# Sending each token once, to its pair of experts, in the last mixture of a vision tower

## The reference, cut to what matters

```python
def _L1_ffn_ref(x, gate_w, gate_b, w1, b1, w2, b2):
    B, S, H, E, K = (8, 1024, 128, 8, 2)
    logits = jnp.einsum('bsh,he->bse', x, gate_w) + gate_b
    topk_vals, topk_idx = jax.lax.top_k(logits, K)
    topk_weights = jax.nn.softmax(topk_vals, axis=-1)
    mask = jax.nn.one_hot(topk_idx, E, dtype=topk_weights.dtype)
    weights = jnp.einsum('bske,bsk->bse', mask, topk_weights)
    h = jax.nn.relu(jnp.einsum('bsh,ehf->bsef', x, w1) + b1)
    expert_out = jnp.einsum('bsef,efh->bseh', h, w2) + b2
    return jnp.einsum('bseh,bse->bsh', expert_out, weights)
...
h = h + _L1_ffn_ref(_layernorm(h, axis=-1), ...)
```

## Time and profile before

| | |
|---|---|
| median of three runs | 1982.61 us |
| the profiled execution: span from its first to its last instruction | 2111.4 us |
| of that: start of the last stage | 1570.6 us |
| routing and wait for the first block | 1570.6 to 1817.8 us |
| blocks, to the last scatter | 1817.8 to 2084.1 us |
| end | to 2111.4 us |
| PE busy | 1779.0 us (84%) |
| DVE, ACT, POOL busy | 1022.5, 833.8, 881.2 us |

### The profile page before, as it was taken

One profiled execution on the slowest core, in us unless ns is written; L12 is line 12 of the kernel. 1 busy time (PEld: TensorE's weight loads), 2 busy tenths in 40 slices (PEclk: granted clock), 3 DMA queues, 4 the chain that ended last, 5 costly groups with the idle time before them and its releaser, 6 DMA issues. The chain is left out here.

```text
span 2111.4 us, 60393 instructions
## 1 busy us (share of the span) xinstructions
PE 1779.0 (84%) x24144; PEld 1295.0 (61%) x24144; DVE 1022.5 (48%) x2949; ACT 833.8 (39%) x2096; POOL 881.2 (42%) x1033
## 2 busy tenths in 40 slices
PE   8999978989999898799989999999883564777772
PEld 3444436767776676387747888888743553666662
DVE  0000057877877777466654555555451112244445
ACT  0000056555655555444455555555450111233331
POOL 0000006877777778001102343334317355365553
PEclk9999989999999999869999999999975555688886
DMA  9878500000000000300000000000012012233445
GB/s 379 314 298 317 203 1 3 4 3 3 3 3 3 3 3 4 89 1 1 1 1 2 2 2 2 2 2 2 2 31 62 26 42 66 72 84 84 122 119 189
DMA packets 68646, 134.75 MB, mean 64 GB/s; under 512 B 12692, under 2 KB 44444, under 8 KB 68412
## 3 DMA queue, kind: packets, MB, share of 16 engines
q1 hardware_dynamic: 57454, 110.68, 15.0%
q0 software_dynamic: 9280, 19.16, 2.7%
q10 hardware_dynamic: 1678, 1.43, 0.2%
HBM read 103.58 MB, written 27.66 MB: 62 GB/s over the span
## 5 line engine op out<-in xcount | busy, mean ns | idle before, releaser
L833 PE MATMUL ps<-xn,s_a_wqkv 128*128 128x260 f32 x1024 | 288.9, 406 | 13.7 <-ACT qk_a L579 7.9
L171 PE MATMUL ps<-x_chunk,s_w_tok 128*128 128x512 f32 x576 | 251.8, 598 | 6.3 <-DMA x_chunk<-in_x_main 6.3
L833 PEld LDWEIGHTS ps<-xn,s_a_wqkv 128*128 128x128 f32 x1024 | 175.9, 192 | 57.3 <-ACT qk_a L579 20.3
L1472 POOL DMA_INDIRECT out_rows<-pad_rows_m,block_goal_m x160 | 154.5, 966 | 131.4 <-DVE pad_rows_m L1803 94.2
L171 PEld LDWEIGHTS ps<-x_chunk,s_w_tok 128*128 128x128 f32 x576 | 109.7, 192 | 147.1 <-issue 147.1
L551 POOL TENSOR_TENSOR prob_a<-e_a,inv_sum_a 128x512 f32<-128x512 f32 x64 | 66.8, 1044 | 246.7 <-DVE inv_sum_a L775 179.7
L1465 POOL DMA_INDIRECT expert_rows<-rows_m,slot_i_m x130 | 125.3, 964 | 98.1 <-DVE slot_i_m L1737 59.7
L652 ACT ACTIVATE e_a<-e_a 128x585 f32<-128x585 f32 (+1 forms) x128 | 85.2, 665 | 182.1 <-DVE e_a L744 93.6
L1557 PE MATMUL ps<-pad_rows_m,s_a_wqkv 128*128 128x256 f32 x320 | 101.5, 447 | 60.9 <-issue 59.5
L481 POOL MEMSET cls_queries_a<- 128x1040 f32 x2 | 1.9, 966 | 345.8 <-POOLq L222 345.8
L591 ACT ACTIVATE resT_a<-ps 128x260 f32<-128x260 f32 x256 | 84.7, 384 | 143.2 <-PE ps L850 120.3
(11 more groups left out here) (247 smaller groups left out, 4422.6 us busy)
## 6 DMA issues: line engine op xcount, KB each, us to landing
x_chunk<-in_x_main SPq DMA_DIRECT2D x96, 768.0 KB, 8.5
s_f_w<-expert_rows SPq DMA_DIRECT2D x40, 130.0 KB
xn<-out_rows SPq DMA_DIRECT2D x13, 320.0 KB
h<-out_rows SPq DMA_DIRECT2D x13, 320.0 KB, 6.3
out<-base_m SPq DMA_DIRECT2D x13, 320.0 KB, 9.1
s_a_wt_t<-expert_rows SPq DMA_DIRECT2D x20, 130.0 KB
s_a_wout<-expert_rows SPq DMA_DIRECT2D x20, 130.0 KB
out_rows<-pad_rows_m,block_goal_m POOLq DMA_INDIRECT x160
```

What stands on the lines that cost most here:

```text
L171: last = nc.tensor.matmul(ps[:, bank, :], w_tok[:, k, :], xb[:, s, k, :], start=(k == 0), stop=False)
L833: nc.tensor.matmul(ps[:, QK_BANK[i], 0:QUAD], w_qkv[:, c * P:(c + 1) * P], xn[:, t.h * QUAD:(t.h + 1) * QUAD], start=True, stop=True).then ...
L1472: nc.gpsimd.indirect_dma_start(acc[g // NB][:, :], bass.IndirectOffsetOnAxis(ap=goal[:, g % R, half:half + 1], axis=0), ys[:, g % R, half, ...
```

## The change

`paired_mixture` takes the place of `sparse_mixture`.

A token now belongs to one of the 28 unordered pairs of experts. Its row is 260 numbers: x, its finished base (h + weighted b2), its name, and the weights of the lower and of the higher expert. It is scattered once, so there are 13 scatters a group, and each now also waits for ACT's copy of the base (`base_sb`), which goes into the row and no longer into `base`. Tiles are 128 adjacent tokens. PE's order of a group is: logits of group g + 1, weights and bases of group g, turn_x and ranks of g + 1.

A block is 128 rows of one pair, and both experts are applied to it. There are 65 slots for full blocks, whose pair comes from a table (computed by DVE with one block per partition, turned by PE onto one partition, copied by DVE), and 28 slots for the last, partly filled block of each pair, whose weights are read in place. ACT copies the turned rows, the lower expert's weights and takes the lower relu; DVE copies the higher expert's weights (at a column it loads itself), takes the higher relu, and adds base + w_lo·y_lo + w_hi·y_hi in two dependent instructions. POOL scatters the finished row to `out`; names of padding rows are out of bounds and are dropped. There are 8 slots for loaded rows, 4 for results. SP puts one of the 28 padding writes after every second load. Accumulators, their loads, the final adds and the store are gone.

```diff
-ROW = D + 2
-BLOCK_ROWS = 256
+ROW = 2 * D + 4
...
+    PAIRS = E1 * (E1 - 1) // 2
+    FULL = tokens // P
+    BLOCKS = FULL + PAIRS
+    RB, RY, RW = 8, 4, 4
...
         def tile_of(t, i):
-            return t[:, i:tokens:TILES]
+            return t[:, i * P:(i + 1) * P]
...
+            for s in range(FULL):
+                load(s)
+                if s % 2 == 1 and s // 2 < PAIRS:
+                    pad_after(s // 2)
...
-                        for t in range(t0, t1):
-                            for k in choices:
-                                nc.gpsimd.indirect_dma_start(
-                                    regions[k][:, :],
...
-            for g in range(K * NB):
-                for half in range(2):
-                    pool.wait_ge(y_done, 2 * g + half + 1)
...
+                for s, (t0, t1) in enumerate(SUBS):
+                    pool.wait_ge(xt_sb, S * g + s + 1)
+                    pool.wait_ge(base_sb, S * g + s + 1)
+                    for t in range(t0, t1):
+                        nc.gpsimd.indirect_dma_start(
+                            region[:, :], bass.IndirectOffsetOnAxis(ap=slot_i[:, g % 2, t:t + 1], axis=0),
+                            rows[:, g % 2, t, :], None).then_inc(sent[g % 2], 16)
+            for s in range(BLOCKS):
+                pool.wait_ge(y_done, s + 1)
+                nc.gpsimd.indirect_dma_start(
+                    out[:, :], bass.IndirectOffsetOnAxis(ap=blk[:, s % RB, NAME:NAME + 1].bitcast(I32), axis=0),
+                    ys[:, s % RY, :], None, bounds_check=tokens - 1, oob_is_err=False).then_inc(added[s % RY], 16)
...
+            def fetch_weights(s):
+                column = dve.value_load(table[0:1, 2, s:s + 1], min_val=0, max_val=WB * (E1 - 1))
+                since(dve, y_ps, s - RW + 1)
+                nc.vector.tensor_copy(wb[:, s % RW, 1, :], w_all[:, :, :].rearrange("p e c -> p (e c)")[
+                    :, bass.ds(column, WB)]).then_inc(w_hi_sb, 1)
...
+            def weigh(s):
+                sl = s % RB
+                dve.wait_ge(y_ps, s + 1)
+                nc.vector.scalar_tensor_tensor(out=half_y[:, s % 2, :], in0=ps[:, 5 + s % 2, 0:D],
+                                               scalar=blk[:, sl, W_LO:W_LO + 1], in1=blk[:, sl, D:2 * D],
+                                               op0=ALU.mult, op1=ALU.add).then_inc(half_done, 1)
+                since(dve, added[s % RY], 16 * (s // RY))
+                dve.wait_ge(half_done, s + 1)
+                nc.vector.scalar_tensor_tensor(out=ys[:, s % RY, :], in0=ps[:, 5 + s % 2, D:2 * D],
+                                               scalar=blk[:, sl, W_HI:W_HI + 1], in1=half_y[:, s % 2, :],
+                                               op0=ALU.mult, op1=ALU.add).then_inc(y_done, 1)
...
+            def step(at):
+                if (s := at(2)) is not None:
+                    relu(s)
+                if (s := at(0)) is not None and s < FULL:
+                    fetch_weights(s)
+                if (s := at(4)) is not None:
+                    weigh(s)
+            pipeline(step)
```

More of the change, by code:

```diff
@@ L1261, in _, with paired_mixture @@
                 nc.gpsimd.tensor_tensor(half(h, i), half(h, i), y[:, i % 2, :], ALU.add).then_inc(h_done, 1)
[L1264 to L1274, removed]
+def paired_mixture(nc, tokens, h, xn, ps, ident, before, all_ones, gate_w, gate_b, expert_ids, w_all, b2, region,
+                   out):
     T = 13
@@ L1315, in sparse_mixture @@
[L1315 to L1325, removed]
@@ L1337, in sparse_mixture @@
[L1337 to L1342, removed]
+        bases = sb("first_row_m", [P, PAIRS])
@@ L1414, in _ @@
[L1414 to L1441, removed]
+            sp.wait_ge(pads_made, 2)
+            sp.dma_start(region[PAIRS * REGION:, :], pad[:, :]).then_inc(pads_in, 16)
@@ L1570, in down @@
+            def down(s):
+                pe.wait_ge(hid_lo, s + 1)
+                pe.wait_ge(hid_hi, s + 1)
+                since(pe, y_done, s - 1)
+                for b, w in enumerate(weights_of(s)):
+                    for f in range(2):
+                        last = nc.tensor.matmul(ps[:, 5 + s % 2, b * D:(b + 1) * D], hid[:, s % 4, b, f, :],
+                                                w[:, F1 + f * P:F1 + (f + 1) * P], start=(f == 0), stop=(f == 1))
                 last.then_inc(y_ps, 1)
@@ L1747, in _ @@
             settle()
-            chained(nc.vector.tensor_reduce(blocks[:, :, :], over[:, :, :, :], AX.X, ALU.add))
+            chained(nc.vector.tensor_scalar(whole[:, :], whole[:, :], WHOLE, None, ALU.add))
             settle()
-            for k in range(K):
-                last = nc.vector.tensor_tensor(part[:, k], blocks[:, k, :].unsqueeze(1).to_broadcast([P, E1, E1]),
-                                               upto[:, :, :], ALU.mult)
-            chained(last)
+            chained(nc.vector.tensor_scalar(part_f[:, :], whole[:, :], WHOLE, float(P), ALU.subtract, ALU.mult))
@@ L1754, in _ @@
             settle()
-            chained(nc.vector.tensor_reduce(end[:, :, :], part[:, :, :, :], AX.X, ALU.add))
+            nc.vector.tensor_copy(part_i[:, :], part_f[:, :])
+            chained(nc.vector.tensor_tensor(full[:, :], part_f[:, :], bases[:, :], ALU.subtract))
             settle()
-            for k in range(K):
-                last = nc.vector.tensor_tensor(past[:, k], number[:, :].unsqueeze(2).to_broadcast([P, NB, E1]),
-                                               end[:, k, :].unsqueeze(1).to_broadcast([P, NB, E1]), ALU.is_ge)
@@ new lines, in relu @@
+            def relu(s):
+                dve.wait_ge(up_hi, s + 1)
+                if s < FULL:
+                    dve.wait_ge(w_hi_sb, s + 1)
+                since(dve, y_ps, s - 3)
+                w = weights_of(s)[1]
+                for f in range(2):
+                    last = nc.vector.tensor_scalar(hid[:, s % 4, 1, f, :], ps[:, 2 + 2 * (s % 2), f * P:(f + 1) * P],
+                                                   w[:, 2 * F1 + f:2 * F1 + f + 1], 0.0, ALU.add, ALU.max)
+                last.then_inc(hid_hi, 1)
```

482 lines of the change are left out of this document (235 added, 247 removed).

## The result

The kernel after takes 1922.3 us (median of four runs, 1918.8 to 1925.22), the kernel before 1982.96 (four runs, 1980.18 to 1983.54). The ratio is 0.9693, 95% interval 0.9676 to 0.9709: 60.7 us less, where 42 were predicted. The profiled execution of after has a span of 1921.9 us, 2 us under that run's own time of 1923.71.

A forecast was written before the change was run, and what follows sets the result against it. POOL's scatters were taken to set the pace of routing and blocks. From 1991 us, 31 for an earlier first block and 26 at the end, less 15 for longer blocks, give 42 gained: 1940 us, range 1865 to 1975 (8 in 10).

The forecast's parts named there:

- the comparison with 1991: Last stage: the profiled 2111 us would end at 1991 if signals weren't noticed late; the changed kernel is compared with that.
- late signals: Routing and blocks: while POOL issues scatters without a pause, other engines notice signals late; explains 120 of 129 us.
- the 8 us: Whole kernel: 1991 us lies 8 us over the timed median; the same 8 us are subtracted at the end.
- most of the late signals belong to the profiled execution: Routing and blocks: the timed runs of before mostly lack the delays, so the gain is 42 us and not 162.
- Routing: Up to the first block: 65 of 130 scatters go, PE sets 27.6 us a group, first block at 1722, against 1753.
- at 1.2 GHz, which is the clock of this stretch: Routing: PE's terms of a group, 27.6 us in sum, were taken at 1.2 GHz (0.54 in the profile).
- DVE is the bound of the 65 full blocks: Full blocks: DVE's terms sum to 2.4 us against PE's 2.0; 2.35 taken, 153 us for 65 blocks.
- The end: After the last scatter: 26 us of loads, additions and stores go entirely, since scatters write the output.
- Late signals real in timed runs: Rival, all scatter bursts over 16 us: the delays also occur unprofiled, gain 152 us, time 1831, or 1886 at half; chance 0.20.
- SP: Rival, blocks: SP's issuing of loads and padding writes becomes the bound, +33 us, time 1973; chance 0.06.
- PE at 1.2 GHz in the blocks: Rival, blocks: PE stays at the lower clock, 3.6 us a block, +120 us, time 2060; chance 0.03.
- Mutual blocking of copy and scatter: Rival, 65 full blocks: DVE's weight copy waits 0.96 us for a POOL scatter in each, time 2006; chance 0.11.

The follow-up runs named there:

- after_third: The kernel after, unchanged, run beside the kernel before on the third chip: 1933.39 us against 2107.97, ratio 0.9171.

## Why the prediction was right, and where it was not

**The bound of before, and the comparison with 1991.** Right in size, wrong in reason. I worked out that without late signals the last stage would end at 1991. On the second chip, whose copies of after show none, the spans of before have a median of 1983.7. So the 8 us were an error of that sum, rightly taken off again; which of its terms was off can't be read, since no trace of before without late signals exists. But the step "most of the late signals belong to the profiled execution" failed: they come with the chip (or its session). That the runs of the result fell where there are none was luck. On the third chip the same change takes 175 us off.

**Routing.** The group's cycle was to be 27.6 us, bound by PE, and was 23.75. PE was the bound, without idle time (busy for 23.69 us of the 23.80 from 1614.6). The terms in the cycle of 1614.6: logits 3.48 (6.15 predicted), weights and bases 15.5 (14.8), turn_x 3.2 (4.1), ranks 1.6 (2.5). The step that failed is "at 1.2 GHz, which is the clock of this stretch". In a cycle in which PE has no idle time, the granted clock rose over ranks and logits and fell for the bases, in each group again (three pieces of a cycle):

```profile
1611.70:1614.60 2.90, 2.90 (x22) 2.44 (x22) 0.00 (x0) 1.46 (x3) 2.29 (x3) 0.72 0.34 119
1614.60:1618.10 3.50, 3.50 (x29) 3.44 (x28) 1.91 (x5) 0.00 (x0) 2.77 (x3) 0.81 0.27 96
1618.10:1633.60 15.50, 15.50 (x67) 12.93 (x64) 6.71 (x60) 3.60 (x8) 6.78 (x7) 0.50 0.17 60
```

The first scatter was late as predicted, 1601.25 against 1595.9, of which 4.7 us come from a stage that starts at 1575.3 and not at 1570.6. The shorter cycles outweigh it: from the first scatter to the fifth group's are 89.0 us, where 4 x 27.6 − 6.15 = 104.3 were predicted. In the fifth group even the bases ran at full clock (1.00 from 1685.1 to 1695.2 us). First block 1711.5, not 1722.

**Blocks.** "DVE is the bound of the 65 full blocks", "without idle time", was wrong: DVE is busy for 73% of them, and PE, busy for 93%, has the longer step. The mis-sized term is the copy of the weights, taken as 0.66 us from ACT's 0.632 and DVE's 0.820 for 640 numbers. That second row is not of a plain copy: L1233 writes each of 5 numbers 128 times (`to_broadcast`). The plain copy measured 0.43 (min/median/max in ns):

```profile
L1793 DVE COPY block_weights_m<-s_f_all x65: 428/430/707, 1696.5 to 1850.4; 128x514 f32 x65
```

With 0.43, my sum for DVE is 2.17 us, and the measured pace is 2.17. That is a coincidence: a second copy of 0.43 us costs only 0.13, so DVE has some 0.3 us of room in a block. PE's own step is 1.87 us, where I took 2.0. Together 141 + 52 us for 209 predicted. Start-up and end were 17.3 us for 18, and that is luck, since two errors cancel. The start-up took 7.3 us (9.5 to the first scatter, less one block) where I took 6 + 8 = 14, although before had only 9.2 to its first scatter. The last scatter and the end took 9.95 us where I took 4. I had left out POOL's closing instruction, 7.6 us of which lie behind the last landing.

**The end.** The loads, additions and stores are gone, as predicted. But they had covered POOL's closing instruction, so the end gave 17.3 us (27.3 − 9.95), where my terms make it 23 (27.3 − 4).

**The sum.** 1921.9 measured, 1949 predicted: 10.5 from the first block, 16.6 from the blocks (210.4 for 227). The 8 us taken off at the end made up for a part of it, so that the forecast missed the median by 18.

**The rivals.** *Late signals real in timed runs*: not for the runs of the result, and real on two of three chips. There the mechanism that the prediction described holds in the main (long bursts bring them, the change takes nearly all away: 4.1 us of waits without a releaser are left in `after_third`, and groups that are 2 us longer), and the gain is 175 us, for which I had 162. *SP*: its loads waited for scatters for 58.7 us, in 59 waits, and held PE up for 5.0. *PE at 1.2 GHz in the blocks*: 0.99 and 1.00. *Mutual blocking of copy and scatter*: scatters went from 0.966 to 1.003 us in the mean, the copy from 0.43 to 0.465 (29.3 us for 63) and at most 0.71. That is 0.07 us a block, where the price was 0.96. The Trainium skill (SBUF — State Buffer, "Who interferes with whom") says that of such a copy and an instruction of GpSimd the one that starts second is blocked for the whole of the other. The trace agrees only in small: 9 of 63 copies take 0.56 to 0.71 us; all nine begin 0.3 to 0.5 us before a scatter ends, and end 0.25 us after it. The other way round, the 15 scatters that begin 0.05 to 0.22 us after a copy take 1.06 to 1.23 us in place of 0.98. But the 25 copies that lie wholly within a scatter take 0.43 to 0.46, no longer than those with no scatter beside them (0.43).

## What to carry to other kernels

When the span of a profile and the times of the runs disagree by more than a few us, ask first whether they come from the same chip, and compare before and after only where both ran. Long runs of scatters from POOL without a pause are a risk even where POOL is the bound anyway: fewer and larger rows (here one of 1040 bytes for two of 520) took the same 0.97 us each. When an engine is freed and PE becomes the bound, take neither PE's durations nor its clock from the stretch in which it was waiting. When the work behind an engine's last instruction goes, look for what else lay beside it: here a closing instruction of 10 us came to light.

## What was not expected of the hardware

- The same program takes 1986 us on one chip and 2106 to 2109 on two others, steadily (13 runs within 0.4%, 34 within 0.9%). The difference shows where POOL issues long runs of scatters one behind the other: the kernel after differs by 10.5 us.
- POOL's closing instruction (DRAIN) takes 10.3 us in before and 10.4 in after, and in after it ends the span 7.6 us behind the last landing.
- A scatter whose rows are all dropped takes POOL as long (0.98 us, 1.29 from start to start) as one that moves 128 rows of 512 bytes, and brings as many packets.
- An fp32 copy of 128x514 from SBUF to SBUF takes DVE 0.43 us and ACT 0.63.
- The granted clock can rise and fall within a 24 us cycle of PE that has no idle time: 0.81 over the logits, 0.50 over the bases.
